# The first attention layer's p times v with high and low parts of v side by side, and its denominators from sums of p

## The reference, cut to what matters

```python
qkv = einsum('oc,bcn->bon', qkv_w, hf) + qkv_b        # q, k, v: 8 heads of 64 x 1024
attn = einsum('bhdi,bhdj->bhij', q, k) * HEAD_DIM ** (-0.5)
attn = softmax(attn, axis=-1)
out = einsum('bhij,bhdj->bhdi', attn, v)
out = einsum('oc,bcn->bon', proj_w, out) + proj_b
return x + out
```

## Time and profile before

| | |
|---|---|
| time, three runs | 2716.35, 2720.72, 2723.38 us; median 2720.72 |
| the profiled execution | span 2718.4 us |
| PE busy | 2619.7 us, 96% |
| DVE busy | 2055.1 us, 76% |
| ACT busy | 1578.5 us, 58% |
| POOL busy | 221.9 us, 8% |
| transfers | 279.48 MB, mean 103 GB/s |

### The profile page before, as it was taken

One profiled execution on the slowest core, in us unless ns is written; L12 is line 12 of the kernel. 1 busy time (PEld: TensorE's weight loads), 2 busy tenths in 40 slices (PEclk: granted clock), 3 DMA queues, 4 the chain that ended last, 5 costly groups with the idle time before them and its releaser, 6 DMA issues.

```text
span 2718.4 us, 33180 instructions
## 1 busy us (share of the span) xinstructions
PE 2619.7 (96%) x11856; PEld 2181.7 (80%) x11856; DVE 2055.1 (76%) x3294; ACT 1578.5 (58%) x1930; POOL 221.9 (8%) x134
## 2 busy tenths in 40 slices
PE   6999999999999999999999999999999987899998
PEld 5788888888888888888888888888888876688887
DVE  6788768876887688768876887688767867878864
ACT  4667646764676467646764676567646663334311
POOL 1000000000000000000000000000000012111010
PEclk9999999999999999999999999999999999899999
DMA  4512232223222322232223222321322335466444
GB/s 156 177 50 80 67 103 61 79 71 100 64 78 67 101 67 76 63 107 67 65 72 109 66 59 79 109 67 48 90 83 58 112 127 203 171 215 246 165 164 170
DMA packets 154849, 279.48 MB, mean 103 GB/s; under 512 B 51776, under 2 KB 52032, under 8 KB 154176
## 3 DMA queue, kind: packets, MB, share of 16 engines
q1 hardware_dynamic: 152128, 268.98, 31.4%
q0 software_dynamic: 2560, 8.39, 1.0%
HBM read 180.04 MB, written 63.18 MB: 89 GB/s over the span
## 4 chain that ended last, share of the span: by engine, by line
PE 83%; DVE 9%; issue 3%; DMA 2%; ACT 1%; SPq 0%; POOL 0%; POOLq 0%; DVEq 0%; ACTq 0%
PE tiles L372 9%; PE tiles L373 8%; PE tiles L374 8%; PE tiles L474 8%; PE tiles L451 8%; PE tiles L428 8%; PE tiles L468 8%; PE tiles L467 8%; PE tiles L447 7%; PE tiles L1321 5%; PE tiles L1371 2%; DVE row_max L679 2%; DVE p_low L695 2%; DVE h_low L787 1%; PE tiles L383 1%
## 5 line engine op out<-in xcount | busy, mean ns | idle before, releaser
L679 DVE TENSOR_REDUCE row_max<-tiles 128x1 f32<-128x512 f32 x1014 | 694.5, 685 | 443.4 <-PE tiles L428 440.6
L544 ACT ACTIVATE p_high<-tiles 128x1024 fp32r<-128x1024 f32 x512 | 525.5, 1026 | 595.8 <-PE tiles L451 595.1
L695 DVE TENSOR_TENSOR p_low<-tiles,p_high 128x1024 fp32r<-128x1024 f32 x512 | 623.0, 1217 | 7.0 <-ACT tiles L546 6.2
L546 ACT ACTIVATE tiles<-tiles 128x1024 f32<-128x1024 f32 x512 | 523.0, 1021 | 0.0
L467 PE MATMUL tiles<-p_high,v_high 128*128 128x512 f32 x1024 | 406.5, 397 | 2.2 <-ACT num_den L562 1.5
L428 PE MATMUL tiles<-k_high_low,q_high_high 128*128 128x512 f32 x1014 | 404.8, 399 | 0.2 <-DVE row_max L679 0.2
L468 PE MATMUL tiles<-p_high,v_low 128*128 128x512 f32 x1024 | 402.0, 393 | 0.0
L428 PEld LDWEIGHTS tiles<-k_high_low,q_high_high 128*128 128x128 f32 x1014 | 312.5, 308 | 48.6 <-DVE row_max L679 5.7
L474 PE MATMUL tiles<-p_low,v_high 128*128 128x512 f32 x1024 | 325.8, 400 | 14.9 <-DVE p_low L695 14.6
L451 PE MATMUL tiles<-q_low_max,k_high_one 65*128 65x512 f32 x1024 | 325.8, 399 | 1.9 <-DMA q_low_max<-row_max_top 1.8
L372 PE MATMUL tiles<-h_high,w_high 128*128 128x512 f32 x768 | 304.6, 397 | 17.3 <-DVE row_max L679 8.3
(11 more groups left out here) (167 smaller groups left out, 3138.1 us busy)
## 6 DMA issues: line engine op xcount, KB each, us to landing
x_tiles<-in_x SPq DMA_DIRECT2D x64, 512.0 KB, 5.4
w_high<-w_split SPq DMA_DIRECT2D x126, 256.0 KB, 2.8
w_low<-w_split SPq DMA_DIRECT2D x126, 256.0 KB, 3.0
k_high_one<-k_high_low SPq DMA_DIRECT2D x128, 128.0 KB, 2.3
q_high_high<-q_high_high SPq DMA_DIRECT2D x128, 128.0 KB, 2.3
o_normed<-rec_rows SPq DMA_DIRECT2D x64, 256.0 KB, 3.7
x<-x_tiles SPq DMA_DIRECT2D x32, 512.0 KB, 4.0
x_full<-x SPq DMA_DIRECT2D x32, 512.0 KB, 8.3
```

Of the source, the lines that this page charges most:

```text
L544: nc.scalar.activation(ph[:, r, :], ring[:, r, :], ACT.Exp, scale=ATT_SCALE).then_inc(s_ph, 1)
L546: nc.scalar.activation(ring[:, r, :], ring[:, r, :], ACT.Exp, scale=ATT_SCALE).then_inc(s_p32, 1)
L679: nc.vector.reduce_max(mcol[:, h % 2, n, i:i + 1], max_bank(h, i, n)[:, :], AX_X).then_inc(s_mx, 1)
L695: tt(pl[:, r, :], ring[:, r, :], ph[:, r, :].bitcast(F32), ALU.subtract).then_inc(s_pl, 1)
```

## The change

v is kept in one tensor `v_parts`: for each head and block of keys 128 columns, the high part of the head's v in one half and the low part in the other (the halves swap for the second head of a pair). There are no columns of ones. The high and the low part of p each meet this weight once, so a block of keys takes two products where it took three, and low x low is added too. The 128 rows are then p times the high part and p times the low part, 64 each; GpSimd issues a transfer that adds the one half onto the other (`add_parts`).

The sums of p are made apart. The full exponential is written to SBUF, to `p_early` in the first two steps of a half head and to `p_late` in the last two. GpSimd issues two transfers that add `p_early` onto `p_late` (`add_early`), adds the four blocks of 512 columns that are left (`fold_late`, `fold_all`), ScalarE copies the high part of the sum (`sums_high`), GpSimd takes the low part (`sums_low`), and TensorE multiplies both with a column of ones (`denominators`), which adds over the keys. ScalarE copies one row of the result (`den_row`). The way from there to `o_normed` is as before, but begins four steps later, and the parting into `o_high` and `o_low` moves with it. The score slot is free once ScalarE has read it twice (`s_p32`). In the first kind of pair the projections are spread like those of the others; seven of the eight output projections go to the next head, and the statistics, stores and loads around them one to two steps later.

```diff
-PAIR_STEPS = (begins(0, 1, 6, 8, 2, 3, 3, 5, whole=(("k", 0), ("k", 1), ("v", 0), ("q", 1))),
+PAIR_STEPS = (begins(0, 3, 6, 8, 10, 12, 12, 14),
...
+            put(b, 7, o[0])
             for s in range(7):
-                put(b, 1 + s, o[s])
-            put(a + 2, 0, o[7])
+                put(a + 2, s, o[1 + s])
...
+def den_half(h, s):
+    return ("d", h - 1, s // 4) if s % 4 == 0 and h > 0 else None
...
+def v_slot(h):
+    return h % 3
...
-    v1 = sb("v_high", [P, 2, NT, 3, HD], F32R)
-    v2 = sb("v_low", [P, 2, NT, 3, HD], F32R)
+    p_late = sb("p_late", [P, 2, N])
+    sum_high, sum_low = (sb(n, [P, HALF], F32R) for n in ("p_sum_high", "p_sum_low"))
+    p_early = sb("p_early", [P, 2, N])
+    vp = sb("v_parts", [P, 3, NT, 2, HD], F32R)
...
+    ones = sb("one_column", [P, 1], F32R)
...
+    def p_full(t):
+        return (p_early if t % 4 < 2 else p_late)[:, t % 2, :]
...
-                pe.wait_ge(s_pl, t - 1)
+                pe.wait_ge(s_p32, t - 1)
...
-        def weights_of(v, t, n):
-            h, j = t // STEPS, 2 * (t % 4) + n
-            return v[:, (h // 2) % 2, j, h % 2:h % 2 + 2, :].rearrange("p a d -> p (a d)")
+        def weights_of(t, n):
+            return vp[:, v_slot(t // STEPS), 2 * (t % 4) + n, :, :].rearrange("p a d -> p (a d)")
         def weigh_high(t):
             if t % 4 == 0 and t > 0:
                 pe.wait_ge(s_vl, vt(("vt", t // (2 * STEPS), 1)))
             pe.wait_ge(s_ph, t + 1)
             for n in range(2):
-                p = ph[:, t % 2, n * HALF:(n + 1) * HALF]
-                mm(pv[:, :], weights_of(v1, t, n), p, start=(t % 4 == 0 and n == 0), stop=False)
-                last = mm(pv[:, :], weights_of(v2, t, n), p, start=False, stop=False)
+                last = mm(pv[:, :], weights_of(t, n), ph[:, t % 2, n * HALF:(n + 1) * HALF],
+                          start=(t % 4 == 0 and n == 0), stop=False)
             last.then_inc(s_phu, 1)
         def weigh_low(t):
             pe.wait_ge(s_pl, t + 1)
             for n in range(2):
-                last = mm(pv[:, :], weights_of(v1, t, n), pl[:, t % 2, n * HALF:(n + 1) * HALF],
+                last = mm(pv[:, :], weights_of(t, n), pl[:, t % 2, n * HALF:(n + 1) * HALF],
                           start=False, stop=(t % 4 == 3 and n == 1))
             last.then_inc(s_plu, 1)
+        def denominators(j, out):
+            pe.wait_ge(s_sumh, j + 1)
+            pe.wait_ge(s_suml, j + 1)
+            one = ones[:, 0:1].broadcast_to([P, P])
+            mm(out, one, sum_high[:, :], start=True, stop=False)
+            mm(out, one, sum_low[:, :], start=False, stop=True).then_inc(s_den, 1)
...
+            d = den_half(h, s)
+            if d:
+                fill_free(d)
+                denominators(2 * d[1] + d[2], banks[BANK[d]][:, :])
...
+            r, j = t % 2, t // 4 - 1
             act.wait_ge(s_sc, t + 1)
             if t > 1:
                 act.wait_ge(s_phu, t - 1)
             nc.scalar.activation(ph[:, r, :], ring[:, r, :], ACT.Exp, scale=ATT_SCALE).then_inc(s_ph, 1)
-            nc.scalar.activation(ring[:, r, :], ring[:, r, :], ACT.Exp, scale=ATT_SCALE).then_inc(s_p32, 1)
+            if j >= 0:
+                if t % 4 < 2:
+                    act.wait_ge(s_acc[t % 2], 16 * (j + 1))
+                elif t % 4 == 2:
+                    act.wait_ge(s_fold, fold((j, "both")))
+                else:
+                    act.wait_ge(s_suml, j + 1)
+            nc.scalar.activation(p_full(t), ring[:, r, :], ACT.Exp, scale=ATT_SCALE).then_inc(s_p32, 1)
+        def sums_high(j):
+            act.wait_ge(s_fold, fold((j, "all")))
+            if j > 0:
+                act.wait_ge(s_den, j)
+            nc.scalar.activation(sum_high[:, :], p_late[:, 1, 0:HALF], ACT.Copy).then_inc(s_sumh, 1)
+        def den_row(j, out):
+            h, i = j // 2, j % 2
+            row = (1 - h % 2) * HD
+            act.wait_ge(s_den, j + 1)
+            act.wait_ge(s_add[i], 16 * (h + 1))
+            nc.scalar.activation(nd[row:row + 1, h % 2, i * HALF:(i + 1) * HALF], out[row:row + 1, :], ACT.Copy
+                                 ).then_inc(s_denrow, 1)
...
-            nc.scalar.activation(v1[:, n % 2, 4 * i:4 * i + 4, 0:3:2, :],
-                                 fill_of(u)[:, :].rearrange("p (j a d) -> p j a d", j=4, a=2),
-                                 ACT.Copy).then_inc(s_vh, 1)
+            if n > 0:
+                act.wait_ge(s_plu, (2 * n - 1) * STEPS)
+            both = fill_of(u)[:, :].rearrange("p (j a d) -> p j a d", j=4, a=2)
+            for a in range(2):
+                last = nc.scalar.activation(vp[:, v_slot(2 * n + a), 4 * i:4 * i + 4, a, :], both[:, :, a, :], ACT.Copy)
+            last.then_inc(s_vh, 1)
...
+            d = den_half(*before(h, s)) if t > 0 else None
+            if d:
+                den_row(2 * d[1] + d[2], banks[BANK[d]])
+            if t % 4 == 3 and t > 4:
+                sums_high(t // 4 - 1)
...
-            if h % 2 == 0 and h > 0 and s == 7:
+            if h % 2 == 1 and h > 1 and s == 5:
...
-            tt(pl[:, r, :], ring[:, r, :], ph[:, r, :].bitcast(F32), ALU.subtract).then_inc(s_pl, 1)
+            tt(pl[:, r, :], p_full(t), ph[:, r, :].bitcast(F32), ALU.subtract).then_inc(s_pl, 1)
...
-                if h % HEADS == 3 and s in (1, 3, 4, 5):
-                    tile_stats(b, (1, 3, 4, 5).index(s))
+                if h % HEADS == 3 and s in (1, 3, 5, 7):
+                    tile_stats(b, (1, 3, 5, 7).index(s))
...
-            if h % 2 == 1 and h > 1 and s == 0:
+            if h % 2 == 1 and h > 1 and s == 6:
                 o_low(h // 2 - 1)
-            if h > 0 and s == 3:
+            if h > 0 and s == 7:
                 reciprocal(h - 1)
...
+            for i in range(2):
+                pool.wait_ge(s_add[i], 16 * (h + 1))
+            pool.wait_ge(s_suml, min(2 * h + 4, 2 * ALL_HEADS))
+            if h > 0:
+                pool.wait_ge(s_on, h)
+            pool.wait_ge(s_rstd, min(max(h + 4, 0) // HEADS + 1, BATCH))
...
+        def add_early(j, n):
+            pool.wait_ge(s_pl, 4 * j + 3 + n)
+            nc.gpsimd.dma_start(p_late[:, n, :], p_early[:, n, :], accum_op=ALU.add).then_inc(s_acc[n], 16)
+        def add_parts(j):
+            h, i = j // 2, j % 2
+            a, cols = h % 2, slice(i * HALF, (i + 1) * HALF)
+            pool.wait_ge(s_nd, j + 1)
+            nc.gpsimd.dma_start(nd[rows_of(a), a, cols], nd[rows_of(1 - a), a, cols], accum_op=ALU.add
+                                ).then_inc(s_add[i], 16)
+        def fold_late(j):
+            pool.wait_ge(s_acc[0], 16 * (j + 1))
+            if j > 0:
+                pool.wait_ge(s_suml, j)
+            if j > 3:
+                pool.wait_ge(s_on, j // 2 - 1)
+            add(p_late[:, 0, 0:HALF], p_late[:, 0, 0:HALF], p_late[:, 0, HALF:N], ALU.add).then_inc(s_fold, 1)
+        def fold_all(j):
+            pool.wait_ge(s_acc[1], 16 * (j + 1))
+            pool.wait_ge(s_fold, fold((j, "late")))
+            add(p_late[:, 1, 0:HALF], p_late[:, 1, 0:HALF], p_late[:, 0, 0:HALF], ALU.add).then_inc(s_fold, 1)
+            pool.wait_ge(s_fold, fold((j, "both")))
+            add(p_late[:, 1, 0:HALF], p_late[:, 1, 0:HALF], p_late[:, 1, HALF:N], ALU.add).then_inc(s_fold, 1)
+        def rstds(j):
+            h = j // 2
+            return min(h // HEADS + (1 if h % HEADS < 4 else 2), BATCH)
+        def sums_low(j):
+            pool.wait_ge(s_sumh, j + 1)
+            pool.wait_ge(s_rstd, rstds(j))
+            add(sum_low[:, :], p_late[:, 1, 0:HALF], sum_high[:, :].bitcast(F32), ALU.subtract).then_inc(s_suml, 1)
...
-        for h in range(1, ALL_HEADS):
+        for h in range(ALL_HEADS):
             b = h // HEADS + 1
-            if h % HEADS == 5 and b < BATCH:
-                rstd(b)
-            normalise(h - 1)
+            for i in range(2):
+                j = 2 * h + i
+                add_early(j, 0)
+                if i == 0 and h > 1:
+                    normalise(h - 2)
+                add_early(j, 1)
+                fold_late(j)
+                add_parts(j)
+                fold_all(j)
+                if i == 0 and h % HEADS == 4 and b < BATCH:
+                    rstd(b)
+                sums_low(j)
+        normalise(ALL_HEADS - 2)
...
-            if h > 0:
-                if s == 2:
-                    den_to_columns(h - 1)
-                if s == 4:
-                    rec_to_row(h - 1)
-                if s == 5:
-                    rec_to_rows(h - 1)
+            if h > 0 and s == 6:
+                den_to_columns(h - 1)
+            if h > 1 and s == 0:
+                rec_to_row(h - 2)
+            if h > 1 and s == 1:
+                rec_to_rows(h - 2)
...
-        order = [("t", 0, t), ("t", 1, t), ("w", 0, t), ("t", 2, t), ("t", 3, t), ("w", 1, t), ("rows", t),
-                 ("t", 0, t + 1), ("t", 1, t + 1), ("o", 0, t), ("o", 1, t), ("t", 2, t + 1), ("t", 3, t + 1)]
```

(17 more changed lines are left out.)

91 lines of the change are left out of this document (55 added, 36 removed).

## The result

The changed kernel takes 3109.9 us (median of 4 runs, 3104.01 to 3117.31) against 2722.05 us before (4 runs): ratio 1.1428, 95% interval 1.1412 to 1.1445. It is slower by 388 us where the forecast said 2619, and the range ended at 2790. The profiled execution's span is 3112.9 us.

The account below looks back on a forecast made before the run. TensorE, at 0.227 us a product, was taken to bound the kernel: 2718.4 - 174.3 (products) + 29 (turn) + 29 (port) + 15 (ends) = 2617, plus 2.3 against the median: 2619 us, range 2550 to 2790.

Parts of the forecast that it names:

- The output projections and the first pair's projections only move: On TensorE, these projections were only put at other steps, so no time was counted for them.
- Products: On TensorE, 1024 products fewer and 256 added, net 768 at 0.227 us: 174.3 us saved.
- D: Landing time of the 512 KB accumulating transfer p_late += p_early, issued by GpSimd: 5.3 us, ends 3.4 and 8.2.
- the port: VectorE's low parts with two SBUF inputs wait for GpSimd: 1.2 us a half head, 29 us lost in all.
- 0.3 us late on 96 half heads: In plain half heads the sum chain's 14.2 us exceeds TensorE's 13.9 us, costing 29 us.
- the turn: Chain of sums from one half head's p_late to the next's: 8.9 us plus the accumulate's landing, 14.2 us.
- It fits, at 94%: VectorE's load of 13.1 us a half head was held to fit into TensorE's 13.9 us.
- ScalarE: Two more copies a half head, 1.2 us at most, 12.1 of 13.9 us in all, hidden by TensorE.
- Ends: Last four half heads without projections 12 us, and the longer chain before the last output projection 3: together 15 us.
- C: Rival: the accumulate is slow and the sum chain sets the pace, slower than before from 6.3 us landing; chance 0.27.
- D, the port for a whole operation: Rival: each low part waits for a whole GpSimd operation, 5.2 us a half head, 2863 us; chance 0.07.
- B: Rival: the sum chain is hidden behind TensorE, 2561 us, or 2590 with the lock loss; chance 0.20.

Follow-up runs that it names:

- the run at 2623 us: Changed kernel with pieces of weights one after another, and accumulates, folds with the subtraction, and row maxima on 8 columns: 2623.0 us, ratio 0.9645.

## Why the prediction was wrong

The first step that failed is "The output projections and the first pair's projections only move", counted at 0. Moved alone they cost the kernel before 270 us (the wait of SyncE that this test added among them), 197 of them by the order of the pieces; in the changed kernel that order costs 142. The forecast counted products and never asked when each piece's load could start and what stands ahead of it in SyncE's queue. Its part on SyncE, which counts 0 as well, asks only after the denominators, the accumulates and the rows of maxima there, not after the weights.

*Products* (-174.3 us): TensorE gives back 0.170 and not 0.227 us a product, by the run with 1024 fewer. At that rate 768 would be 131 us, an estimate.

*D* (5.3 us, measured 4.8) and the port (1.2 us a half head, measured 1.19) were right in size. Their prices were not: 29 us each, against 96 for the accumulates and, in the run with the low part in PSUM, 67 for the port, with the folds at 95 in all. The step that failed there is "0.3 us late on 96 half heads": it weighs one long turn, which ends where ScalarE waits for GpSimd's subtraction, against TensorE's half head. That wait is small; the large one is at the accumulate (us in all, times, longest):

```profile
ACT p_early L592 <- DMA p_late<-p_early: 301.1, 169, 9.0
...
ACT p_late L592 <- POOL p_sum_low L999: 65.8, 78, 1.5
```

The path behind the large one is shorter than the turn, and the sum has no term of its own for it (the forecast says of the exponential's wait for transfers: "that is in the turn"). The exponential of step 0 may overwrite p_early only when an accumulate has landed that itself waits for the low part of step 2, two steps before; 251 of the 301 us are at step 0. In the changed kernel, from the exponential of step 2 to that of step 0:

```profile
879.67 1.02 ACT L592 ACTIVATE p_late<-tiles 128x1024 f32<-128x1024 f32 x1
...
882.53 2.37 POOL L999 TENSOR_TENSOR p_sum_low<-p_late,p_sum_high 128x512 fp32r<-128x512 f32 x1
882.54 1.22 DVE L766 TENSOR_TENSOR p_low<-p_late,p_high 128x1024 fp32r<-128x1024 f32 x1
...
884.85 0.92 POOL L967 DMA_DIRECT2D p_late<-p_early  x1
...
889.74 1.03 ACT L592 ACTIVATE p_early<-tiles 128x1024 f32<-128x1024 f32 x1 [1.45 <-DMA p_late<-p_early]
```

These two steps take 10.07 us, where two of four in 13.9 us are 6.95. The low part stands behind a maximum that waits for its product, the issue stands behind GpSimd's subtraction, which meets the low part and takes 2.37 us, and the landing takes 4.9. What the wait costs is shown (75 us with p_early doubled); how it is shared out among these links is not. In the turn itself GpSimd's term was too small as well, since the port holds GpSimd too: "three make 3.9", measured 1.30 (median), 1.73 and 1.61 us (means), 4.6 in all.

*"It fits, at 94%"* of VectorE failed too: with the sums all but gone, shorter maxima still gave 147 us. At that load, in a fixed order against another engine as full and with two slots of scores between them, TensorE did not keep its pace here.

*ScalarE* was counted as hidden. What stands behind its waiting exponential is also the copy that empties the one bank of p times v: TensorE's products of the high part waited 38.2 us for it (1.5 in the kernel before).

*Ends* (15 us, 10 of them work that gets longer): from the last copy to the end 518.5 us (2594.4 to 3112.9) against 504.5, 14 more where 3 were counted; the last four half heads 61.9 us against 47.6, 14 more where 7 were counted.

The rivals: C had the sign of the result, and its own sign was half there: ScalarE is idle for a transfer 2.35 us a half head on the mean, over 2 us in 64 of 128. By C's condition, D above 6.3 us, the chain should not have decided; at 4.8 the accumulates still cost 96 us. D, the port for a whole operation (low parts near 2.5 us), did not come as the rule but in single cases (2.46 us above). B is refuted: TensorE is 86% busy from 600 to 900 us and not 99%.

The miss is 491 us. Steps from run to run account for 142 by the weights, 198 - 58 = 140 by accumulates and folds beyond the forecast, and 147 by VectorE's room: 429. The shares hold for this order of reliefs only, for each gain depends on what was relieved before. Open are 62. Of these, 11 lie behind the last copy: 14 us more, of which 3 were counted, and the run at 2623 us has them too. The 43 us that fewer products gave less may be the same missing room on VectorE as the 147; that is not shown.

By the Trainium skill (DMA: Bandwidth & Descriptors, Anatomy of one DMA — SWDGE (gpsimd) path) the estimate for D was 4.4 us; the median of 4.8 is nearer to it than to the 5.3 of the rows, and it decided nothing.

## What to carry to other kernels

A unit that is moved takes its loads with it: list which pieces are open at each step, how many slots hold them, and what stands ahead of the next load in its queue, before calling a move free. When the bounding engine is relieved by a sixth, read the next one's load at the new pace, and do not take 94% in a fixed order for a fit: here it was none. For every buffer that is written again, follow the shortest path from its last writer over its readers to the next write, in steps, and not only the longest chain: the wait that cost most in the sums was at p_early, two steps long. Reliefs measured one by one under a larger stall were too small here (79 and 44 us), so remove the largest stall first, and measure again (96 and 95).

## What the runs showed of the hardware

The accumulating transfer of 512 KB landed in 4.5 us at best, 4.8 in the median and 12.1 at worst in the changed kernel; its issue took GpSimd 0.876 us. The port holds GpSimd as well: the last fold took 1.26 to 2.34 us, its median 1.87, where the two before it had medians of 1.28 and 1.30 on the same shape. And a gap of 5.31 us on TensorE was followed by 4 us of products at half speed (granted clock 0.52), so late weights were paid for twice.
